# Moments of the first layer norm four chunks ahead, and absolute sums of two weight matrices taken in eight quarters

## The reference, cut to what matters

```python
xn = _layernorm(x, axis=-1)              # x: 2 x 2048 rows of 256
s = _L0_attn_ref(xn, ...)                # sigmoid attention, q and k layer-normed
g = _silu(_L0_ffn_ref(xn, ...))          # 16 routed experts, 4 of them per row, and a shared expert
x = x + s * g
xn = _layernorm(x, axis=-1)
s = _L1_attn_ref(xn, L1_attn_k, L1_attn_v)
g = _silu(_L1_ffn_ref(xn, L1_ffn_W1, L1_ffn_b1, L1_ffn_W2, L1_ffn_b2))
x = x + s * g

def _layernorm(x, axis=-1, eps=1e-05):
    m = jnp.mean(x, axis=axis, keepdims=True)
    v = jnp.var(x, axis=axis, keepdims=True)
    return (x - m) / jnp.sqrt(v + eps)

def _ternary(w):                         # in _L1_ffn_ref, for W1 (1024 x 256) and W2 (256 x 1024)
    scale = jnp.maximum(jnp.mean(jnp.abs(w)), 1e-08)
    w_t = jnp.clip(jnp.round(w / scale), -1.0, 1.0)
    return w + jax.lax.stop_gradient(w_t - w)
```

## Time and profile before

| | us |
|---|---|
| median of three runs (lowest, highest) | 1265.87 (1263.99, 1266.9) |
| the profiled execution, its own time | 1265.47 |
| its span, first to last instruction | 1263.6 |
| PE busy in it | 1215.7 |
| DVE busy in it | 892.7 |
| first norm, from the start to the first product of the shared expert | 45.9 |
| DVE waiting for POOL's powers in the first norm (15 to 42 us) | 3.6 |
| the two sums of absolute values on DVE (408 to 414 us) | 2 x 2.28 |

### The profile page before, as it was taken

The page is one execution under the profiler, slowest core; times in us unless marked ns, Lnnn a source line. Parts: engine busy times, 40 slices in busy tenths (PEclk is TensorE's granted clock), DMA queues, the critical chain, the costliest instruction groups (busy, mean ns, idle before and its releaser), DMA issues.

```text
span 1263.6 us, 26659 instructions
## 1 busy us (share of the span) xinstructions
PE 1215.7 (96%) x8985; PEld 868.5 (69%) x8986; DVE 892.7 (71%) x1906; ACT 555.4 (44%) x1044; POOL 426.7 (34%) x391
## 2 busy tenths in 40 slices
PE   4899999999999999999999999999999999999998
PEld 4445666777688788866666667777766666666665
DVE  7798767566467766668899898999765455545554
ACT  6433643333256566656333334666632222222221
POOL 2232677776409360035777761331000000000000
PEclk8899999999999999999999999999999999999999
DMA  9898323333388666631466666342121011101100
GB/s 287 244 368 331 125 95 107 130 126 109 105 256 257 176 193 190 191 98 45 142 192 194 180 196 227 118 136 84 42 77 50 1 51 51 50 0 50 50 18 17
DMA packets 134063, 169.22 MB, mean 134 GB/s; under 512 B 12197, under 2 KB 121914, under 8 KB 131674
## 3 DMA queue, kind: packets, MB, share of 16 engines
q1 hardware_dynamic: 117386, 130.21, 32.1%
q0 software_dynamic: 12368, 33.70, 8.3%
q10 hardware_dynamic: 4224, 4.19, 1.0%
HBM read 84.18 MB, written 83.89 MB: 133 GB/s over the span
## 4 chain that ended last, share of the span: by engine, by line
PE 80%; DVE 8%; issue 6%; POOL 3%; DMA 2%; ACT 1%; SPq 0%; DVEq 0%; POOLq 0%; ACTq 0%
PE bank L1191 28%; PE sums L1238 24%; PE bank L1117 7%; PE sums L1205 4%; PE sums L1127 4%; PE bank L1097 2%; PE bank L1034 2%; PE sums L1366 2%; PE sums L1050 1%; DVE reg_e L2075 1%; POOL xg_d L821 1%; PE sums L1040 1%; PE sums L1069 1%; PE bank L1160 1%; PE bank L1059 1%
## 5 line engine op out<-in xcount | busy, mean ns | idle before, releaser
L2085 DVE TENSOR_SCALAR reg_w<-reg_w 128x512 f16<-128x512 f32 x320 | 147.0, 459 | 219.0 <-ACT reg_w L1590 218.4
L1238 PE MATMUL sums<-reg_v,reg_w 128*128 128x256 f16 x2304 | 282.4, 273 | 0.0
L1238 PEld LDWEIGHTS sums<-reg_v,reg_w 128*128 128x128 f16 x2304 | 225.4, 98 | 66.2
L1768 DVE SCALAR_TENSOR_TENSOR reg_w<-reg_w 128x512 f16<-128x512 f32 x320 | 223.3, 698 | 11.0
L1191 PE MATMUL bank<-reg_qk 128*128 128x512 f16 (+1 forms) x768 | 186.6, 379 | 0.0
L1191 PE MATMUL bank<-reg_qk,kbT 128*128 128x512 f16 (+1 forms) x768 | 186.6, 379 | 0.0
L1590 ACT ACTIVATE reg_w<-bank 128x512 f32<-128x512 f32 x128 | 76.4, 597 | 245.1 <-PE bank L1191 245.0
L1590 ACT ACTIVATE reg_w<-bank,nlogs 128x512 f32<-128x512 f32 x128 | 88.0, 688 | 179.3 <-PE bank L1191 172.9
L844 POOL DMA_INDIRECT reg_e<-yg_d,slot_i x128 | 131.0, 1024 | 46.5 <-issue 34.1
L839 POOL DMA_INDIRECT xg_d<-xr,icol x108 | 110.0, 1019 | 47.9 <-issue 25.9
L1191 PEld LDWEIGHTS bank<-reg_qk,kbT 128*128 128x128 f16 x768 | 75.1, 98 | 63.3
(11 more groups left out here) (241 smaller groups left out, 1740.0 us busy)
## 6 DMA issues: line engine op xcount, KB each, us to landing
xg_d<-kbT SPq DMA_DIRECT2D x18, 1024.0 KB, 5.3
xin<-xg_d SPq DMA_DIRECT2D x72, 256.0 KB, 2.8
yg_d<-xr SPq DMA_DIRECT2D x72, 256.0 KB, 2.2
reg_qk<-in_L_attn_x_dram SPq DMA_DIRECT2D x8, 512.0 KB, 8.3
sh_d<-xin SPq DMA_DIRECT2D x16, 256.0 KB, 3.1
xr<-xn_d SPq DMA_DIRECT2D x32, 128.0 KB, 2.3
reg_e<-sh_d SPq DMA_DIRECT2D x32, 128.0 KB, 2.7
moe_d<-reg_e SPq DMA_DIRECT2D x32, 128.0 KB, 1.9
```

Source lines behind the costliest of these rows:

```text
L1238: mm = pe.matmul(a_bank[2 * i + q // 2][:, (q % 2) * D:(q % 2 + 1) * D], part[:, j % 4, q * P:(q + 1) * P], m.second(y, j), start=(j == 0 ...
L1768: ins = dve.scalar_tensor_tensor(out=out_ap, in0=in_ap, scalar=scale, in1=hi_ap, op0=ALU.mult, op1=ALU.subtract)
L2085: dve.tensor_scalar(ah[:, j % 4, :], att[:, j % 2, :], m.split, None, ALU.mult).then_inc(m.hi_done, 1)
```

## The change

The moments of chunk 3 and of chunk 4 are both taken at the end of iteration 0, and from then on iteration c ends with the moments of chunk c + 4 instead of c + 3; iterations 4 to 7 have none. The work is the same, its place is not. In the routed experts each matrix is summed in four quarters of 128 x 512, one in each of the steps 18 to 25, into eight columns of `mv` (idle in this stage). In step 25 one small reduction of 128 x 8 adds the quarters to the two columns of `thr` from which POOL takes them; POOL now waits for nine signals instead of two. The last sum moves from step 27 to step 31, and 32 steps are written out instead of 28.

```diff
-                pool.wait_ge(tn_sum, 2)
+                pool.wait_ge(tn_sum, 9)
...
-                if c < NCH - 3:
-                    x_moments(c + 3)
+                if c == 0:
+                    x_moments(3)
+                if c < NCH - 4:
+                    x_moments(c + 4)
...
+                quarter_sums = mv[:, :, :, :].rearrange("p a m q -> p (a m q)")[:, 0:2 * G4]
+                quarters = [quarter_sums[:, n:n + 1] for n in range(2 * G4)]
...
-                    if isinstance(c, int) and c in (20, 21):
-                        dve.wait_ge(ld["w12"], 16 * 8)
-                        dve.tensor_reduce(thr[:, c - 20:c - 19], st_w[c - 20], AXX, ALU.add, apply_absolute_value=True
+                    if isinstance(c, int) and 18 <= c < 18 + len(quarters):
+                        if c == 18:
+                            dve.wait_ge(ld["w12"], 16 * 8)
+                        n, q = divmod(c - 18, G4)
+                        dve.tensor_reduce(quarters[c - 18], st_w[n][:, q * 512:(q + 1) * 512], AXX, ALU.add,
+                                          apply_absolute_value=True).then_inc(tn_sum, 1)
+                    if isinstance(c, int) and c == 25 and len(quarters) == 8:
+                        dve.wait_ge(tn_sum, 8)
+                        dve.tensor_reduce(thr[:, 0:2], quarter_sums.rearrange("p (n q) -> p n q", q=G4), AXX, ALU.add
                                           ).then_inc(tn_sum, 1)
-                    if isinstance(c, int) and c == 27:
+                    if isinstance(c, int) and c == 31:
...
-                by(dve, NSLOT_T // 2, 4, one_step, head=28)
+                by(dve, NSLOT_T // 2, 4, one_step, head=32)
```

## The result

The changed kernel takes 1259.8 us (median of six runs, 1258.95 to 1261.7) where the kernel before, run beside it, takes 1265.28 us (six runs, 1263.99 to 1266.9). The ratio is 0.9964, with a 95% interval of 0.9954 to 0.9974: 4.6 us less by the ratio, 5.5 us by the medians. Forecast were 1261.0 us, 4.7 us less.

What follows compares the result with a forecast made beforehand. PE, busy 1215.7 of 1263.6 us, was taken as the bound, held up by DVE in two places. First norm 2.4 plus sums 2.3 gave 4.7 us less than 1265.47: 1260.8, told as 1261.0, range 1258.2 to 1264.2.

Steps and rivals of the forecast that it cites:

- The shift's wait: First norm: DVE idles for POOL's power before writing the shift; 0.67 us a round to be had, 0.59 in some.
- The double group: First norm, iteration 0: moments of two chunks taken together cost DVE 1.97 us more, putting chunk 3's shift at 21.2.
- The ring at the end: First norm's end: shift, ACT's norm, transposes, rounding, low half, next shift take 3.45 us; chunk 7's shift 2.4 us earlier.
- The cover of chunk 4 of x: First norm: chunk 4 lands at 17.4, DVE comes for it at 18.6, so 1.2 us cover the load.
- The sums: Routed experts: the two long reductions cost 2.3 us; eight quarters of 0.6 us fit DVE's idle time, gaining 2.3 us.
- The slack of PE: Routed experts: about 0.4 us of DVE's lateness reaches nobody, since PE's longest wait was shorter than that lateness.
- The gap at "issue": Routed experts: PE stood 1.2 us reading the experts' numbers behind the slow steps; some may go, widening the range by 0.5.
- POOL's ternary weights: Routed experts: POOL starts on them about 8 us later; they are wanted only in the second half's attention, over 100 us on.
- The rival of the small gain in the first norm: First norm: the wait for POOL becomes one for ACT or PE; 0 to 0.7 us left of 2.4; 12%.
- Each quarter pays: Routed experts: a quarter at 0.69 us outlasts the 0.62 us idle time; eight cost 0.56 us, time 1261.4; 10%.
- The clock: First 50 us and shared expert: another stretch of PE at 0.50 costs 1.7 us, or 3.4; 1262.7 to 1264.4; 15%.
- Slower: Shared expert: PE held at 0.50 after an emptier first norm, 14.4 us more than before; 1268.4 us; 3%.

Runs made afterwards that it cites:

- moments alone: Kernel before with the first norm's moments four chunks ahead and the two long reductions kept: 1261.36 us, ratio 0.998.
- the halves: Kernel before with the sums as four reductions of 128 x 1024, one in each of steps 18 to 21: 1263.58 us, ratio 0.999.
- the doubled ones: Kernel before with the sums in eight quarters, each reduced twice in its step, the second result unread: 1317.21 us, ratio 0.9998.
- the other ways of placing the shift: Kernel before, shift behind both low halves: 0.9982, with quarters 0.9965; changed kernel, shift ahead of both from chunk 1: 0.9971, also chunk 2's behind both: 0.9958.
- before again: The kernel before, unchanged, run once more on the third chip: 1319.65 us, ratio 0.9993.
- change for the third time: The changed kernel, nothing further altered, run on the third chip against the kernel before: 1313.54 us, ratio 0.9946.

## Why the prediction was right

**The shift's wait: right, a little too small.** Taken were 0.67 us a round. Measured is a round of 3.83 us (22.03 to 25.86) where it had been 4.55: 0.72. The prediction took 0.66 us from the start of a low half to the shift behind it, and by its own 1.30 that makes 0.64, not 0.67; the rows after the change have 0.60 (21.43 to 22.03). The double group cost 1.96 for 1.97. With the moments alone, where chunk 2 landed as before, the shift of chunk 3 stood at 21.26, said were 21.2, and that of chunk 7 at 36.75, said were 36.9.

**The ring at the end: right.** It takes over at the shift of chunk 7, as the low half that ACT releases at 36.89 shows. It lasts 3.38 us (34.12 to 37.50), put at 3.45. The part brought 2.65 us for 2.4: 0.05 more in each round and 0.07 in the ring. L1059, put near 43.5, came at 43.31 with the moments alone and at 44.06 in the change, whose stage began 0.8 us late. Behind the shift of chunk 7 nothing moved: 6.54 us to L1059 before, 6.56 after.

**The cover of chunk 4 of x held:** the second group, at 19.46, has no idle time ahead of it. So did that of step 18: its reduction at 399.19 follows its low half at once.

**The sums: right.** 2.3 us were said, and 2.3 us are gone: the five steps that took 15.47 us take 13.18 (399.89 to 413.07). A quarter was put at 0.6 us and costs 0.59 to 0.60; its reduction is 0.68 us long, as said. The slack of PE, put at 0.4 us, is 0.47 by the halves. That the gain hangs on idle time, step by step, is shown by the traces of the same eight quarters in two steps (203.4 us for the stage, no gain) and of the doubled ones (201.1, about half of it); their times alone are too wide for it.

**The gap at "issue": left out of the sum, and it came.** It was said that some of the 1.2 us may go, up to 0.5. It lies at 1.05 to 1.17 us in the seven traces whose DVE is late in the steps ahead, and at 0.61 to 0.71 in the seven with one quarter a step. With it the second part is worth 2.3 + 0.5 = 2.8 us. The bound of 2.8 was right and the value of 2.3 too cautious. Why PE's reading is slow behind late steps isn't shown, and late steps aren't the only cause: the like gap twelve steps earlier lies at 0.54 to 1.37 us with no reduction ahead of it.

**POOL's ternary weights** were to come "about 8 us later". Counted from step 18 their last instruction ends 7.7 us later, but since step 18 itself is 3.7 us earlier, it is only 3.9 us later (463.4 before, 467.3 now), far ahead of the second half's attention.

**The rival of the small gain in the first norm** fell: the ring over ACT ended one round, not all. **Each quarter pays** fell too. The rule of the Trainium skill told in the prediction ("VectorE: DVE Perf Modes", the TRN2 errata) gives the length of the instruction well, an estimated 0.69 us for 0.68 measured; but the next instruction starts 0.59 to 0.60 us after it, and in a full row of work that is the cost.

**The clock** was a rival, and it comes and goes from one execution of the same kernel to the next. The stretch of the earlier trace rows at 46.6 us was priced at 1.7 us; on the way to L1069 it is worth 1.4 to 1.5 (13.23 or 13.22 against 11.76 to 11.79). Of the stretch of 10.2 us only 5.6 us lie behind the first L1059 (45.5 to 51.1), and they were worth 2.4 (14.18). So the 1.44 us in the profiled execution can't be booked to the change. Whether the order of the moments makes such a stretch rarer stays open: it fell behind the gate in five of six traces with the old order, in one of four with the order of the change, and in three of four with the other ways of placing the shift.

**The sum: right, its closeness partly luck.** By cause 2.65 + 2.8 = 5.5 us are accounted for, 0.25 and 0.5 more than the two terms that were forecast, and 5.5 is also the difference of the medians. The 4.6 us of the ratio lie within 0.1 us of the forecast 4.7, but their interval goes from 3.3 to 5.8 us and holds both.

**Slower** fell: PE wasn't at 0.50 for longer behind the gate in any run of the change (at most 3.4 us, as before).

## What to carry to other kernels

A big job on an engine that isn't the bound should be cut to the idle time that each turn of the loop has, and spread over turns: here eight pieces of 0.6 us in idle times of 0.62 us cost nothing, the same eight in two turns cost as much as the whole did, and four pieces of 1.13 us cost 0.8 us of PE's steps where the whole had cost 2.3. Where an engine asks another for a result and wants it one instruction later, some work between the two is enough: one instruction moved behind another gave 2.7 to 2.8 us, as much as moments one chunk further ahead. Before a gain is put down to an edit, the traces of the kernel before should be several: here a stretch of low clock worth 1.4 us came and went with one and the same kernel.

## What the runs showed of the hardware

- The cost and the length of a DVE reduction of absolute values differ by a like amount at all sizes: 512 elements 0.68 us long, 0.60 from start to start; 1024 elements 1.21 and 1.13; 2048 elements 2.28 and 2.19. From start to start, 512 elements more cost 0.53 us, so an instruction by itself costs an estimated 0.06 to 0.07 us, worked out from these three. Four of 512 in a row take 2.37 us (410.70 to 413.07 with the quarters in two steps), 0.18 more than one of 2048, as three such costs would make.
- PE's granted clock goes up and down in the first 50 us in every trace, at other times each. The Trainium skill ("TensorE: Matmul & The Clock Gate", Part 1) has 1.2 GHz as the default that sustained activity lifts; the 0.50 of the rows above is that level, and the traces agree as to busy stretches: from 60 to 1240 us, with PE seldom idle, no window of 20 us is under 0.99 in the kernels before and after and the one with the moments alone, on the first chip. On the third, windows between 620 and 820 us go down to 0.83 (before again, change for the third time), in the stage where PE stands still more often (last point), and one from 340 to 360 us is at 0.91 in the latter, behind a wait of PE of 2.4 us.
- The landing of one chunk of x shifts the whole first norm: the moments of chunk 2 start anywhere from 11.42 to 13.38 us in the fourteen traces, and from there to the gate it takes 33.87 to 33.93 us in all six with the old order.
- The second and the third chip need 52 and 56 us more for the same program. In the traces 50 to 53 of them lie in the second half's attention, from the first L1205 to the first L1238 behind it: 185.3 us in the kernel after on the first chip (590.2 to 775.5), 235.1 on the second. Results are gathered row by row there: from 560 to 780 us POOL waits 12.4 us for DVE to have used gathered rows in the kernel after on the first chip, and 57.6 us on the second. The first lines of the waits there, 560 to 780 us, of the change on the second chip:

```profile
POOL reg_e L844 <- DVE reg_e L2088: 57.6, 12, 6.9
ACT reg_w L1590 <- remote: 44.2, 9, 10.8
```

  The program is the same on both. What makes the stage slower on two of the chips wasn't tried and stays open.
